# A graph-and-router network on one core: the router's and the gather's steps in another order, and constants multiplied on TensorE in between

## The reference

```python
    xn = _layernorm(x, axis=-1)
    x = x + _L0_gnn_ref(xn, edge_index, ...) + _L0_mix_ref(xn[None], ...)[0]
    x = x + _L0_ffn_ref(_layernorm(x, axis=-1)[None], ...)[0]
    xn = _layernorm(x, axis=-1)
    x = x + _L1_gnn_ref(xn, edge_index, edge_attr_64, ...) + _L1_mix_ref(xn[None], ...)[0]
    x = x + _L1_ffn_ref(_layernorm(x, axis=-1)[None], ...)[0]

    def _L0_ffn_ref(x, switch_w, switch_b, expert_w, expert_b):
        ...
        logits = xf @ switch_w.T + switch_b
        probs = jax.nn.softmax(logits, axis=-1)
        route_probs = jnp.max(probs, axis=-1)
        routes = jnp.argmax(probs, axis=-1)
        oh = jax.nn.one_hot(routes, E, dtype=jnp.int32)
        pos = jnp.take_along_axis(jnp.cumsum(oh, axis=0), routes[:, None], axis=1)[:, 0] - 1
        capacity = int(CAPACITY_FACTOR * N / E)
        keep = pos < capacity
        buf = jnp.zeros((E, capacity, D), dtype=xf.dtype).at[routes, pos].set(xf)
        y = jnp.einsum('ecd,efd->ecf', buf, expert_w) + expert_b[:, None, :]
        gathered = y[routes, jnp.minimum(pos, capacity - 1)]
        out = jnp.where(keep[:, None], gathered, xf) * route_probs[:, None]
        return out.reshape(B, S, D)
```

## Time and profile before

| | |
|---|---|
| median of three runs | 861.49 us (861.15 to 863.32) |
| the profiled execution, its device time | 859.79 us |
| its span, from first to last instruction | 858.0 us |
| busy: PE, DVE, ACT, POOL | 775.5, 616.8, 381.5, 117.2 us |
| mean granted TensorE clock, share of full speed | 0.96 |

### The profile page before, as it was taken

The page is one execution under the profiler, slowest core; times in us unless marked ns, Lnnn a source line. Parts: engine busy times, 40 slices in busy tenths (PEclk is TensorE's granted clock), DMA queues, the critical chain, the costliest instruction groups (busy, mean ns, idle before and its releaser), DMA issues. The chain is left out here.

```text
span 858.0 us, 11649 instructions
## 1 busy us (share of the span) xinstructions
PE 775.5 (90%) x4058; PEld 572.3 (67%) x4058; DVE 616.8 (72%) x1225; ACT 381.5 (44%) x583; POOL 117.2 (14%) x91
## 2 busy tenths in 40 slices
PE   4989999999999982699599999899989999999998
PEld 3777887888778861465287777665556566665876
DVE  7777887776758757698864424288986888898646
ACT  2342343343214412375321202855632888887453
POOL 3000000000000005010454000444340013000000
PEclk9999999999999995699589999999999999999999
DMA  5563322310302142999320301100000000010002
GB/s 183 155 204 114 100 74 58 89 41 8 123 0 99 50 176 98 264 377 317 108 99 1 99 0 50 50 0 2 1 2 3 3 1 1 1 56 2 1 1 98
DMA packets 48152, 66.63 MB, mean 78 GB/s; under 512 B 4268, under 2 KB 22460, under 8 KB 48095
## 3 DMA queue, kind: packets, MB, share of 16 engines
q1 hardware_dynamic: 43903, 56.22, 20.3%
q0 software_dynamic: 2384, 6.92, 2.5%
q10 hardware_dynamic: 1808, 2.75, 0.9%
HBM read 56.38 MB, written 9.50 MB: 77 GB/s over the span
## 5 line engine op out<-in xcount | busy, mean ns | idle before, releaser
L974 PE MATMUL bank<-xT,slot 128*128 128x512 f32 (+1 forms) x248 | 107.2, 432 | 2.7 <-DVE xT L1782 2.3
L975 PE MATMUL bank<-xT,slot 128*128 128x512 f32 (+1 forms) x248 | 99.0, 399 | 0.0
L976 PE MATMUL bank<-xT,slot 128*128 128x512 f32 (+1 forms) x248 | 98.5, 397 | 0.0
L1485 ACT ACTIVATE slot<-bank 128x512 fp32r<-128x512 f32 (+3 forms) x60 | 34.2, 586 | 137.7 <-PE bank L1241 56.3
L974 PE MATMUL bank<-slot 128*128 128x512 f32 (+1 forms) x212 | 83.2, 392 | 5.2 <-DVE slot L1782 1.9
L974 PE MATMUL bank<-slot,xT 128*128 128x512 f32 (+1 forms) x192 | 78.7, 410 | 2.8 <-DVE slot L2296 1.9
L976 PE MATMUL bank<-slot 128*128 128x512 f32 (+1 forms) x212 | 80.8, 381 | 0.0
L975 PE MATMUL bank<-slot 128*128 128x512 f32 (+1 forms) x212 | 80.8, 381 | 0.0
L2321 DVE TENSOR_REDUCE key<-bank 128x2 f32<-128x1024 f32 x64 | 74.3, 1218 | 6.9 <-PE bank L1301 6.9
L976 PE MATMUL bank<-slot,xT 128*128 128x512 f32 (+1 forms) x192 | 76.1, 396 | 0.0
L975 PE MATMUL bank<-slot,xT 128*128 128x512 f32 (+1 forms) x192 | 75.9, 395 | 0.0
(11 more groups left out here) (339 smaller groups left out, 1637.3 us busy)
## 6 DMA issues: line engine op xcount, KB each, us to landing
arena<-in_ewT SPq DMA_DIRECT2D x16, 1024.0 KB, 11.1
arena<-in_edge_attr SPq DMA_DIRECT2D x16, 512.0 KB, 3.9
wraw<-in_qkvT SPq DMA_DIRECT2D x3, 1024.0 KB, 5.1
expert_rows<-rows SPq DMA_DIRECT2D x1, 2560.0 KB, 13.8
wraw<-in_L_ffn_expert_b POOLq DMA_DIRECT2D x16, 160.0 KB, 5.9
expert_results<-wraw ACTq DMA_DIRECT2D x16, 160.0 KB, 5.7
xn<-in_x SPq DMA_DIRECT2D x4, 512.0 KB, 6.9
wraw<-in_L_mix_w_qkv SPq DMA_DIRECT2D x2, 1024.0 KB, 8.1
```

Source lines behind the costliest of these rows:

```text
L974: pe.matmul(out, L[1], R[0], start=start, stop=False, **kw)
L975: pe.matmul(out, L[0], R[0], start=False, stop=False, **kw)
L976: return pe.matmul(out, L[0], R[1], start=False, stop=stop, **kw)
L1485: act.activation(h, src, kw.pop("func", ACT.Copy), **kw).then_inc(hi_done, 1)
```

## The change

It has seven parts.

1. **Bias on ACT.** The router's bias is loaded as a column and added by ACT when it copies the transposed logits, so `choose` begins with the maximum, read from the bank. Five DVE operations lead to the one-hot matrix (now bf16); the rest follows behind it.
2. **Counts on PE.** `tot0` is gone. `cum0` of a half is one product with the triangular matrix and several with ones over the tiles before, all in bf16 into one bank; those that need only the first half stand ahead of the wait for the second. `place` is five DVE operations; what only the gather needs comes after the second half's indices.
3. **Order of tile 7.** DVE normalises tile 7 ahead of the low parts of tiles 4 to 6, and ACT takes its root ahead of their high parts. The second half's logits are two groups of twelve matmuls: 384 columns for tiles 4 to 6, then 128 for tile 7.
4. **POOL.** Two of the first four bias loads go ahead of the eight indexed stores.
5. **Work moved out of the gather.** `aggT` is transposed ahead of `eY` 14, evicted by ACT, its row of ones is set by POOL, and its weights are loaded once expert 14's weights are split. The split of W1a stands on ACT ahead of the last store; that of W2a stands on DVE behind the low parts of tiles 2 and 3. ACT takes the root of tiles 2 and 3 ahead of all four high parts.
6. **Splat parameters.** 15 small DVE operations (L2173 to L2187) move from the router stage to behind the first `HW` products.
7. **`keep_awake`.** PE multiplies the identity by 512 columns of the constant table, fp32, into a bank that nobody reads: three times when the second half's indices are made, twice when the eight indexed stores have landed, three times when the first gathered row has landed, twice when the fourth has.

```diff
@@ plan_jobs, routed_attention_steps
+        if e == EXPERTS - 1:
+            for g in range(2):
+                add("aggT", g, bank=2 + g)
         if e > 0:
             add("eY", e - 1, bank=6 + (e - 1) % 2)
+    for t in range(TH):
+        add("xT", 2, t, bank=4 + t)
     turn[0] = 0
-    add("aggT", 0)
-    add("aggT", 1)
-    for t in range(TH):
-        add("xT", 2, t)
...
-    return steps + [("xT", 1, 4), ("xT", 1, 5), ("xT", 1, 6), ("cum0", 0), ("tot0", 0), ("xT", 1, 7),
-                    ("lT", 0, 1), ("rt0", 1), ("cum0", 1), ("tot0", 1)]
+    return steps + [("xT", 1, 4), ("xT", 1, 5), ("xT", 1, 6), ("cum0", 0), ("xT", 1, 7),
+                    ("lT", 0, 1), ("rt0", 1), ("cum0", 1)]
@@ SP
-            finished(sp, "eY", EXPERTS - 1)
+            sp.wait_ge(ew_split, 2 * (EXPERTS - 1))
             sp.dma_start(w1e[0:EA], a["L1_gnn_W1"][D:D + EA]).then_inc(w1e_in, 16)
@@ POOL
+            load_bias(0)
+            load_bias(2)
             for t in range(T):
...
+            load_bias(1)
+            load_bias(3)
+            for e in range(4, EXPERTS):
+                emptied(pool, "eY", e - 4)
+                load_bias(e)
+
+            pool.wait_ge(ew_split, 2 * (EXPERTS - 1))
+            pool.memset(aggT[EA:EA + 1, :], 1.0).then_inc(blk_ready, 1)
@@ PE
+            def keep_awake(b, times):
+
+                for _ in range(times):
+                    pe.matmul(bank[:, b, :], ident, kst[:, 0:512], start=True, stop=True)
...
+                    for lo_, hi_ in (((0, TH),), ((0, TH - 1), (TH - 1, TH)))[th]:
+                        for t in range(lo_, hi_):
+                            emptied(pe, "xT", 1, th * TH + t)
+                        w = slice(lo_ * P, hi_ * P)
+                        for k in range(C):
+                            ins = mm3(o[0:EXPERTS, w], hl(swP, k), hl(xT[th], k, w), k == 0, k == C - 1)
...
+                    if th:
+                        for d in range(TH, T):
+                            pe.matmul(o[:, (d - TH) * EXPERTS:TH * EXPERTS], ones16, tiles(0, T - d), start=d == TH, stop=False)
                     pe.wait_ge(onehot_ready, th + 1)
+                    pe.matmul(o[:, 0:TH * EXPERTS], tri16_first, tiles(th * TH, (th + 1) * TH), start=th == 0, stop=False)
...
+            pe.wait_ge(route_ready, 2)
+            keep_awake(3, 3)
+            pe.wait_ge(rows_sent, 16 * T)
+            keep_awake(3, 2)
...
+            emptied(pe, "eY", EXPERTS - 2)
+            pe.wait_ge(gathered[0], 16)
+            keep_awake(bank_of[("eY", EXPERTS - 2)], 3)
+            pe.wait_ge(gathered[3], 16)
+            keep_awake(bank_of[("eY", EXPERTS - 2)], 2)
             for t in range(TH):
                 turn_rows(2, t)
@@ ACT
+            act.wait_ge(ew_split, 2 * (EXPERTS - 1))
+            for g in range(2):
+                finished(act, "aggT", g)
+                act.activation(aggT[0:EA, g * HALF:(g + 1) * HALF], at("aggT", g)[0:EA, :], ACT.Copy)...
             send_y(act, EXPERTS - 2)
+            split_weight("W1a")
             send_y(act, EXPERTS - 1)
-            split_weight("W1a")
             split_weight("W2a")
@@ DVE, router
-                    if s == T - 2:
-                        normalise(1, 1, lambda t: xres[:, t, :])
+                    if s >= T - 2:
+                        normalise(1, s - T + 3, lambda t: xres[:, t, :])
...
+                dve.tensor_tensor(Z, by_tile(cum), chosen[:, w], ALU.mult).then_inc(evicted[bank_of[cum]], 1)
                 emptied(dve, *cum)
+                link(dve.tensor_reduce(c_d[:, w], Z, AX, ALU.add))
+                link(dve.tensor_tensor(c_g[:, w], c_d[:, w], c_h[:, w], ALU.add))
+                link(dve.scalar_tensor_tensor(c_f[:, w], c_d[:, w], float(CAP), c_g[:, w], ALU.is_lt, ALU.mult))
+                dve.tensor_tensor(idx[:, 0, w], c_f[:, w], kst[:, K_TOK + th * TH:K_TOK + (th + 1) * TH], ALU.add)...
@@ DVE, gather
             split_weight("W1a")
-            split_weight("W2a")
-            for g in range(2):
-                finished(dve, "aggT", g)
-                dve.tensor_copy(aggT[0:EA, g * HALF:(g + 1) * HALF], at("aggT", g)[0:EA, :])...
-            dve.memset(aggT[EA:EA + 1, :], 1.0).then_inc(blk_ready, 1)
...
+            routed(TH)
+            normalise(2, 1, lambda t: xres[:, t, :])
             for t in range(2):
                 lo(("xT", 2, t))
-            normalise(2, 1, lambda t: xres[:, t, :])
-            routed(TH)
+            routed_moments(TH)
             for t in range(2, TH):
                 lo(("xT", 2, t))
+            split_weight("W2a")
```

155 lines of the change are left out of this document (74 added, 81 removed).

## The result

The changed kernel takes **849.1 us** (median of 4 runs, 848.1 to 856.4; the kernel before on the same chip: 861.9, 861.2 to 863.3), a ratio of **0.9863, 95% interval 0.9836 to 0.9891** (which is not simply the ratio of the two medians, 0.985): 12.8 us by the medians where 6.1 were predicted. The profiled execution took 848.3 us, its span 846.5. A second set of six runs gave 849.0 and 0.9846 (0.9817 to 0.9875).

A forecast was written before the change was run, and what follows sets the result against it. PE is busy 775.5 of 858.0 us, so time lies where it waits (17.95 and 9.20 us) or runs at the lower clock. Router 5.0 plus gather 1.1 is 6.1 us off 861.49: 855.4, range 850.5 to 859.0.

The forecast's parts named there:

- step 2 of the router: Second half's logits on PE: run at the half clock level, 5.2 us, ending at 326.2, a gain of 1.3.
- The rival: Router: logits run at full level because shorter pauses keep the clock up; 2.2 us more, 853.2; chance 0.18.
- Four stores, 6.6: POOL, router's second half: four stores take 6.6 us, against 6.80 before and a floor of 5.1.
- The rows, 5.45: Experts' rows, SP's issue to PE: 6.03 us before, shortened by 0.55 through two bias loads no longer ahead.
- The loop stays: Experts' loop: itself unchanged, first expert's products at half level; interval to the last eY 55.7 to 56.4 us.
- a sign of being wrong: Experts' loop: the prediction counts as wrong if the loop takes longer than before.
- To the first gather, 5.45: Last eY to first gather: aggregates' transposes ahead of eY 14 add 0.65 us, gathers from 410.65 against 410.01.
- From there to `H`, 17.90: Gather stage: H starts about 18 us behind the first gather's issue, at 428.55, 1.1 us sooner.
- The last store did not wait for W1a: Rival, before the gathers: last store waits for ACT's W1a split, each us past 404.6 delaying gathers by one; chance 0.06.
- GpSimd is not slow by itself: Rival, POOL's stores and gathers: GpSimd slow by itself, second-half stores 1.96 us each, 858.9; chance 0.12.
- `keep_awake` does, at best, half of what it is called: Rival: clock is up when first expert's products and H begin, 6.5 us more, 848.9; chance 0.08.
- Behind `H`, nothing either way: Behind first HW products: the 15 moved splat operations take 3 us where DVE waits anyway; no gain or loss.

The follow-up runs named there:

- before_bias: The kernel before with only two of the four first bias loads moved behind the eight indexed stores; medians differ by 3.8 us (interval 2.0 to 5.4).
- order7: no_const with the old order around tile 7 and the second half's logits in one group; medians differ by 1.9 us.
- ew6_early: The changed kernel with the seventh expert's weights issued ahead of SP's wait for the indexed stores; 849.7 us.
- few_bias: The changed kernel plus three constant products directly ahead of H, without twelve bias loads in the experts' loop; 847.8 us (844.6 to 853.2).
- gap_only: The changed kernel with three constant products directly ahead of H and none of the change's ten; 847.5 us.
- no_const: The changed kernel without its ten constant products, its waits kept; 851.5 us.
- router_const: The changed kernel with only the router's five constant products, the gather's five left out; 851.0 us.
- w2a_early: no_const with DVE's split of W2a back directly behind that of W1a, ahead of the routed rows; 851.5 us.
- router_only: no_const with the whole gather stage as before the change; the rearranged gather stage is worth 2.5 us by the medians.
- before: The kernel before the change, on the same chip; 861.9 us (861.2 to 863.3).
- before_const: The kernel before with only the router's five constant products added; ratio 1.0002.

## Why the prediction was wrong, point by point

The mechanisms of the rearrangement held, and five of ten links were hit within about 0.5 us: the logits' start, the chain behind them, SP's issue, and the two links from the first gather to `H`. Two went the other way: the logits and the wait for the first gather were to take longer (5.30 for 4.59, 5.45 for 4.80) and took less (2.96 and 3.55). Nine of the ten erred to the same side, and all ten come to 7.93 us. The 2.5 us lost behind `H`, which the prediction had at nothing, hid a third of that.

1. **The logits' length is the step that failed most**: step 2 of the router, "I take the half level, 326.2 [...] and keep 324.0 for the range". They ran at the full one, 2.96 us, worth 2.34 more. The rival had 0.18; the runs give it 9 of 13. I had seen that the pause was now split by transposes, and set against it that the level fell behind 2.79 us. But the pauses were 1.67 and 1.23, and I had no row on what such short ones do.
2. **Four stores, 6.6: they took 5.85.** The reason given was only half right. The slow stores do lie beside DVE's splits (before, the last one beside the additions of L2170 too), but not all that lie beside them are slow: the splits run from 329.38 on, the second store overlaps them from there and the third (330.42 to 331.45) entirely, and they took 0.97 and 1.03 us; only the fourth took 1.97. It is so in all thirteen executions with the new order of stores and splits. What decides which one is slowed stays open. 0.75.
3. **The rows, 5.45: they took 4.27.** Of a bound from zero to 1.4 I took 0.55 without a row that spoke for it; `before_bias` shows all of it (1.50). 1.18. Bytes over rate was the estimate to take.
4. **The loop stays: it did (55.17 for 55.78)**, but for another reason than one bound. The first expert gained what I had said it would not, since its products ran at the full level and not "at the half level as now", and waits for weights took it back: behind the first expert the loop was 1.95 us longer, which the prediction had listed as a sign of being wrong.
5. **To the first gather, 5.45: 3.55.** I had charged 0.65 for the aggregates' transposes ahead of the last expert's products. They cost 0.2: in the four kernels that have them there and no waits for weights late in the loop (`order7`, `ew6_early`, `few_bias`, `gap_only`) the last two bias additions lie 2.17 to 2.19 us apart, where it was 2.02, and those before them 3.27, as before. The other 1.25 is the last result's store: issued as soon as its bias is added, it has landed, and the first gather starts, 2.87 us after that addition where it was 4.11. This link is 3.55 to 3.67 us in ten of the kernels with changes and 4.15 to 5.02 in `no_const`, `router_const`, `w2a_early` and `router_only`. I have no experiment on it, and its cause stays open. One thing in the traces goes with it, the aggregates' weights (256 KB), which part 5 asks for sooner. In `before`, `before_const`, `before_bias` and `router_only` SP issues them just ahead of the last store (405.21 and 405.93 in `before`), and the link is 4.80 to 5.02 us. Asked for some 6 us ahead of it, they have arrived by 0.5 us behind the store's issue in the ten kernels with 3.55 to 3.67 us. In `no_const`, `router_const` and `w2a_early` it was 0.2 to 1.3 us behind it, so the two groups are not cleanly apart.
6. **From there to `H`, 17.90: 17.17.** The contention of split and gather was right and is now tested (1.3 us). The constants ended at 409.5, with the clock raised at 407.3, 4.5 us after they began, as the prediction read it from the earlier trace rows; tile 0 was ready at 408.0, so they were late by 1.4 us, and `H` did not feel it.
The Trainium skill, "TensorE: Matmul & The Clock Gate", Part 1, was weighed here. It has sustained activity release the clock. The constants agree, and the aggregates' products on 65 rows disagree again: 6.58 us of them without a pause (L1281 above) did not raise the level, which had fallen 0.7 us after they began.
7. **The rivals.** The last store did not wait for W1a: ACT issued it at 395.65, 0.04 us behind the end of its bias addition. GpSimd is not slow by itself. `keep_awake` does, at best, half of what it is called and is worth nothing as placed.
8. **Behind `H`, nothing either way: 2.5 us were lost.** The granted clock dipped there (last section).

The range did add its unknowns up: its lower end was 855.4 less 2.2 for the logits, 0.85 for the rows and 1.85 for the rest. The first two came with 2.34 and 1.18. For the rest the links show 4.4 us (1.9 to the first gather, 0.75 of the stores, 0.6 of the loop, 1.15 in the other five), of which the 2.5 lost behind `H` took more than half back. Without that loss, for which the prediction had no reason, the measured time would lie some 4 us under the range and not 1.4, so that it is this near is luck. Nearly every unknown was bounded on one side by "as now", and in this case nearly all came out on the other.

## What to carry to other kernels

A constant product is worth something only directly ahead of the work that it is for, and if no second bound takes the gain back: with 0.84 us behind the last one the level held and gave 2.5 us, with 2.77 it was lost. A path of ten hand-overs is worth shortening even where each link saves only about a us, and the small loads that stood in a queue ahead of the one that everybody waits for cost their full bytes over rate (1.5 us for 320 KB). Before you count a gain ahead of a loop, look for the second bound of the loop: here DVE at 48.2 us and the weights at up to 51.
